# Issuing the next expert's input transposes ahead of, not behind, the current expert's first products in a mixture-of-experts tail

## The reference, cut to what matters

```
a_e = top2_idx.reshape(-1)                       # expert of each pick
keep = counts <= cap                             # cap = 320
buf = zeros((E, cap+1, H)).at[a_e, p].set(x_a)   # tokens sorted by expert
h = silu(einsum('ech,efh->ecf', buf, w1) + b1)   # 320 x 256 by 256 x 256, per expert
y = einsum('ecf,egf->ecg', h, w2) + b2           # the same again
```

## Time and profile before

| | us |
|---|---|
| runs | 1271.47, 1274.42, 1276.09 |
| median | 1274.42 |
| the profiled execution, its own time | 1271.47 |
| its span, first to last instruction | 1269.4 |
| mean granted clock of TensorE | 0.885 of full |

### The profile page before, as it was taken

The page is one execution under the profiler, slowest core; times in us unless marked ns, Lnnn a source line. Parts: engine busy times, 40 slices in busy tenths (PEclk is TensorE's granted clock), DMA queues, the critical chain, the costliest instruction groups (busy, mean ns, idle before and its releaser), DMA issues.

```text
span 1269.4 us, 19930 instructions
## 1 busy us (share of the span) xinstructions
PE 1015.9 (80%) x8500; PEld 763.2 (60%) x8500; DVE 579.0 (46%) x1328; ACT 356.8 (28%) x491; POOL 228.7 (18%) x234
## 2 busy tenths in 40 slices
PE   6989689989888888888875797888879797974860
PEld 3656566666657777787874564756556474643540
DVE  3544443544683421111113834655573659445227
ACT  2443323433441121111111243142315323330112
POOL 0310210210212223222221010101000110102642
PEclk9888888888988999999997996999699789965985
DMA  5012922012005787777762000200020010004426
GB/s 168 2 38 79 347 60 67 1 38 67 1 1 200 273 293 279 281 263 259 264 252 82 1 6 2 67 2 5 1 67 2 5 34 1 2 1 136 144 85 198
DMA packets 68216, 129.22 MB, mean 102 GB/s; under 512 B 12752, under 2 KB 57696, under 8 KB 63136
## 3 DMA queue, kind: packets, MB, share of 16 engines
q1 hardware_dynamic: 45984, 97.85, 22.6%
q10 hardware_dynamic: 16480, 14.62, 3.7%
q0 software_dynamic: 5664, 15.47, 3.4%
HBM read 94.50 MB, written 33.42 MB: 101 GB/s over the span
## 4 chain that ended last, share of the span: by engine, by line
PE 53%; DVE 22%; DMA 13%; ACT 6%; issue 2%; POOL 2%; SPq 1%; ACTq 1%; another core or an unknown queue 0%; POOLq 0%; DVEq 0%
DMA sb_arena<-in_m_w 10%; PE ps L1627 7%; PE ps L1324 6%; PE ps L1443 6%; DVE sb_arena L793 6%; PE ps L1509 5%; PE ps L1419 4%; ACT sb_arena L587 4%; DVE sb_arena L797 3%; PE ps L1637 3%; DVE ps L816 3%; PE ps L1562 2%; PE ps L1465 2%; PE ps L1701 2%; PE ps L1451 2%
## 5 line engine op out<-in xcount | busy, mean ns | idle before, releaser
L1627 PE MATMUL ps<-sb_arena 128*128 128x128 f32 x1248 | 160.0, 283 | 42.4 <-DMA sb_arena<-in_m_w 41.8
L1627 PEld LDWEIGHTS ps<-sb_arena 128*128 128x128 f32 x1248 | 149.8, 197 | 56.3 <-DMA sb_arena<-in_m_w 55.3
L1214 POOL TENSOR_TENSOR sb_arena<-sb_arena,sb_neghalf 128x2 f32<-128x2 f32 x40 | 30.4, 761 | 600.5 <-DVE sb_arena L759 600.5
L587 ACT ACTIVATE sb_arena<-ps 77x2048 f32<-77x2048 f32 (+1 forms) x64 | 118.5, 1874 | 54.7 <-PE ps L1401 42.8
L1324 PE MATMUL ps<-sb_arena,sb_wreg 128*128 128x256 f32 (+1 forms) x512 | 106.9, 361 | 4.6 <-issue 3.8
L1324 PEld LDWEIGHTS ps<-sb_arena,sb_wreg 128*128 128x128 f32 (+1 forms) x512 | 88.5, 194 | 19.4 <-issue 8.3
L1419 PE MATMUL ps<-sb_arena 32*77 32x256 f32 (+1 forms) x1024 | 93.8, 496 | 6.8 <-ACT sb_arena L587 4.0
L1112 DVE COPY sb_arena<-ps 128x256 f32<-128x256 f32 x39 | 16.5, 424 | 158.9 <-PE ps L1621 158.9
L822 DVE RECIPROCAL sb_arena<-ps 128x32 f32<-128x32 f32 x24 | 8.6, 357 | 147.3 <-PE ps L1451 146.4
L1637 PE MATMUL ps<-sb_arena 128*128 128x256 f32 x312 | 73.9, 380 | 0.6 <-ACT sb_arena L688 0.6
L1273 POOL DMA_INDIRECT outs<-sb_arena,sb_idx x39 | 38.3, 983 | 194.1 <-ACT sb_arena L688 194.1
(11 more groups left out here) (228 smaller groups left out, 1717.8 us busy)
## 6 DMA issues: line engine op xcount, KB each, us to landing
sb_arena<-in_m_w SPq DMA_DIRECT2D x39, 1536.0 KB
sent<-sb_xres SPq DMA_DIRECT2D x32, 256.0 KB, 2.9
sb_arena<-outs SPq DMA_DIRECT2D x16, 512.0 KB, 5.6
outs<-sb_zeros ACTq DMA_DIRECT2D x1, 6656.0 KB, 32.7
sent<-sb_zeros ACTq DMA_DIRECT2D x2, 2560.0 KB, 12.8
sb_arena<-in_m_w SPq DMA_DIRECT2D x16, 256.0 KB
early<-sb_xres SPq DMA_DIRECT2D x12, 256.0 KB, 2.9
sb_arena<-in_xT SPq DMA_DIRECT2D x8, 256.0 KB, 3.4
```

What stands on the lines that cost most here:

```text
L587: nc.scalar.activation(dst, src, ACT.Exp).then_inc(S(f"h_PT{p}"), 1)
L1214: g.tensor_tensor(b.rstd, b.var, neghalf[:, 0:NT], ALU.pow).then_inc(S(f"{n}_rstd{p}"), 1)
L1627: ins = mm(to[:, m * P:(m + 1) * P], w[:, k, m * P:(m + 1) * P], slots0[j % 2].xT[:, k, :], start=(k == 0), stop=(k == KC - 1))
```

## The change

Two lines move up within PE's loop over the experts. The transposes of expert `e + 1` are issued at the head of the loop body, ahead of the waits and first products of expert `e`. Nothing else differs: the same instructions, tiles, banks and semaphores, and the other four engines have the same instruction streams.

```
             turn1(0)
             for e in range(E):
                 b = experts1[e % XBUFS]
+                if e + 1 < E:
+                    turn1(e + 1)
                 pe.wait_ge(S(f"t_w{e % XBUFS}"), weights_at(e))
                 pe.wait_ge(S("e_xT"), e + 1)
...
                         ins = mm(ps[:, 2 + m, 0:CAP], b.w1[:, k, m * P:(m + 1) * P], xT1[:, k, CAP * e:CAP * (e + 1)],
                                  start=(k == 0), stop=(k == KC - 1))
                     ins.then_inc(S("e_u"), 1)
-                if e + 1 < E:
-                    turn1(e + 1)
                 pe.wait_ge(S("e_h"), KC * (e + 1))
```

## The result

| | before | the change |
|---|---|---|
| median of 22 runs each, us | 1274.91 | 1281.27 |
| lowest and highest | 1258.41 to 1284.74 | 1275.09 to 1286.59 |
| ratio, 95% interval | | 1.0066 (1.0044 to 1.0089) |
| the profiled execution, us | 1271.47 | 1270.34 |
| its span | 1269.4 | 1268.3 |

The change is slower, as forecast, but by more than forecast: 4.18 us would be 0.33%, and the ratio says 0.66%. By the medians the loss is 6.4 us, by the ratio 8.4 us. The profiled execution of the change, however, is 1.1 us faster than that of the kernel before. So the two profiles can't explain the difference of the medians. They can show what happened to each step.

The account below looks back on a forecast made before the run. PE, with 53% of the chain, was taken to bound the kernel. Bare transposes, 1.98 + 1.32 + 0.88 = 4.18 us, on the median 1274.42 gave 1278.6 us; range 1273.5 to 1282.5, the forecast's own 1276.5 to 1280.5.

Parts of the forecast that it names:

- The gap of the Silu: Between first and second products PE waits 0.62 us for the Silu, whether or not transposes stand there.
- The warm sets: Transposes of experts 2 to 7 laid bare at full clock: 3 x 0.66 = 1.98 us and 3 x 0.44 = 1.32 us.
- The cold set of expert 1: Four transposes ahead of expert 0's first products at half clock: 0.88 us, bounds 0.44 and 2.5 us.
- The moved waits: Waits for gathers and DVE's copy, moved with the transposes, cost nothing; tightest gather, expert 4's, has 2.4 us of slack.
- The clock: By the skill's rule the new 0.62 us gaps would be dear; the trace does not bear it out.
- The sum: Bare transposes of experts 1 to 7 together: 1.98 + 1.32 + 0.88 = 4.18 us slower, chance 0.60.
- the two long waits: Second products of experts 3 and 4 start 2.23 and 2.16 us late; with a cold set 5.97 us, left unchanged.
- rival 1: Late signals at experts 3 and 4 do not recur: saves 5.97, pays 4.18, so -1.8 us, 1272.6; chance 0.12.
- Rivals 3 and 4: 3: every new gap cools the clock, 26 us, 1300, chance 0.03. 4: transposes hide at new place, 1274.4, chance 0.09.
- Rival 2: One more cold stretch, at expert 3 or expert 0's start: 5.8 or 6.4 us, 1280.2 to 1280.8; chance 0.16.

Follow-up runs that it names:

- e1: The changed kernel with four unused transposes of the identity matrix in each gap ahead of the second products: ratio 1.0035 to the kernel before.
- e7: The kernel before with one transpose for each of experts 1 to 7 instead of six or four, at the old place: ratio 0.9991.
- p1: The kernel before with a short POOL addition, about 0.7 us, ahead of each gather in the loop: ratio 1.0009 to the kernel before.
- c1: The kernel before, unchanged, timed against itself and profiled a second time: ratio 1.0009.
- e4: The kernel before with PE one expert deeper (first products e + 1, transposes e + 2, second products e) and DVE reordered to match: ratio 1.0011.
- q: Pair q1 and q2, old and changed order with POOL quiet: the change costs 3.9 us by the ratios, 3.1 by the medians.
- p: Pair p1 and p2, old and changed order with POOL pauses: the change costs 3.6 us by the ratios, 2.5 by the medians.
- c3: The changed kernel, unchanged, measured once more against the kernel before: ratio 1.0022.
- c5: The changed kernel, unchanged, in the fourth batch against the kernel before: ratio 1.0047.
- c4: The changed kernel, unchanged, measured a fourth time against the kernel before: ratio 1.0014.
- e2: The kernel before with PE one expert deeper (first products e + 1, transposes e + 2, second products e), DVE's order left: ratio 1.0163, 21 us slower.
- q1: The kernel before with all 20 gathers ahead of POOL's loop and all scatters behind the last expert: ratio 1.0218.
- q2: The changed kernel with all 20 gathers ahead of POOL's loop and all scatters behind the last expert: ratio 1.0249 to the kernel before.
- g1: The kernel before with all 20 gathers ahead of POOL's loop, scatters left in the loop: ratio 1.0066.
- p2: The changed kernel with a short POOL addition, about 0.7 us, ahead of each gather in the loop: ratio 1.0037 to the kernel before.
- c2: The changed kernel, unchanged, in the first batch against the kernel before: ratio 1.0037.
- e3: The changed kernel with expert 1's transposes back behind the first products of expert 0: ratio 1.0011 to the kernel before.
- e5: The changed kernel with each set of transposes of experts 1 to 7 issued twice at the new place: ratio 1.0043 to the kernel before.

## Why the prediction was right and wrong

**The gap of the Silu.** Right: it is 0.62 us at experts 1 to 7 of the undisturbed change, and the same with four transposes in it (e1) or with one (e7).

**The warm sets.** Forecast 3.30 us. Between the second products of expert 0 and those of expert 7 the change takes 1225.75 - 1181.37 = 44.38 us, p1 1221.63 - 1180.41 = 41.22: 3.16 us. Six transposes cost 0.61 us where I took 0.66, four cost the 0.44 that I took.

**The cold set of expert 1.** Forecast 0.88 us. The second products of expert 0 start 8.34 us behind the first transposes, against 7.60 before and 7.59 in p1, but 8.01 in c1: 0.3 to 0.75 us. In the profile of the change the clock rose at about 1178.9, inside the first products, so these did not run cold to their end and took a part of it back.

**The moved waits.** Right: no idle time ahead of the transposes beyond DVE's copy at expert 0. The slack in the gathers is real but finite; the deeper order of e4 used it up.

**The clock.** The new gaps of 0.62 us lie at full clock, and no set behind them was slower. That such gaps would be dear was the prediction's own step from the rule that it named: the section of the Trainium skill (TensorE: Matmul & The Clock Gate, HAM oscillation) describes a loop in which each wait for a DMA is longer than the 2 us or so of matmuls ahead of it.

**The sum.** The undisturbed rows give 3.3 to 3.9 us, where the forecast was 4.18. By ratios, the pairs with an equal edit on POOL give 3.9 us (q) and 3.6 us (p), and the four later direct comparisons 1.8 to 6.0 us; by medians all of these are lower, 3.1, 2.5 and 0.8 to 4.9 us. So the mechanism and its size hold in the rows. The first measurement, 6.4 to 8.4 us, is one and a half times to twice the forecast. Its median of 1281.27 us still lies in the stated range, but by that range's width, which was drawn for late signals and cold sets, and not by the forecast's own, which ended at 1280.5.

**The step that failed** is in the passage on the two long waits: "so I leave this loss as it is". I took the 5.97 us of late signals as a fixed share of every execution of both kernels, and so as nothing in the sum. In the very next profile, that of the change, the loss was zero. That is the sign of rival 1, and the pair of profiles followed it (-1.1 us of span), but the medians did not. Profiles of the unchanged kernel had 6.0 us of it (57.81 against the 51.82 of p1) and then none (c1); profiles of the change had 0, 0, 4.1, 3.9 and 5.3 us. It also seems to come by batches. The medians of the kernel before were 1269.2 and 1270.0 us in the two batches whose profiles with POOL's usual or paced order have no late signals, and 1275.2 to 1278.0 us in the three with them. A term of the size of the whole effect, which comes and goes, should have widened the forecast's own range and not been set to cancel.

That late signals made the first 22 runs of the change worse by the missing 2.5 to 5 us is possible; it is not shown. What lifted that one measurement stays open. Two other sources of scatter are as large. Over all profiles the first transposes started between 1172.1 and 1179.7 us, behind the same PE code. And within one kernel the longer executions were mostly those with the lower granted clock: of the change, 1286.59 us at 0.875 and 1270.34 us at 0.892. The clocks of the kernel before in that first comparison are on record for the profiled execution only, so this can't settle it.

**The rivals.** Rivals 3 and 4 are out by the rows. Rival 1 came true in the pair of profiles and not in the medians. Rival 2 happened in part: where late signals came, sets of 4.28 and 4.65 us stood behind them in c3 and c5, and none in c4 or in the undisturbed profiles.

## What to carry to other kernels

Work that fills a wait has no price until it is moved: ask of each instruction what else could stand in its gap, and whether its new place has one. When an order is deepened, every engine that feeds it must be reordered with it, and its slack in transfers counted again. And a loss seen in one profiled execution is first to be looked for in a second one of the same kernel before it is added to or left out of a sum.

## What the runs showed of the hardware

Signals from TensorE to ScalarE and VectorE can arrive several microseconds late while GpSimd issues indirect DMAs on end. Thirteen profiles have the usual order of DMAs (all but e2, e4, q1, q2, g1, p1 and p2). In nine of them single sets of second products started late, after waits of 0.86 to 5.61 us. All stood at experts 2 to 5, and never at 6 and 7, where GpSimd pauses. With 20 gathers in a row the wait was 9.3 to 12.2 us (q1, q2, g1).

Unbroken issuing is not enough for it. In c1, c2, e1 and the profile of the change it lasted 28 us and nothing was late. Nor does the chip alone decide: the first two batches ran on the same one, the first without late signals in c1, c2 and e1, the second with them in c3, e3 and e5. Full DMA engines don't explain it either. Their mean busy share was 0.9 or more in eight of the 52 one-microsecond stretches from 1180 to 1232 us both in the disturbed kernel before and in the undisturbed c2, while it was 0.18 to 0.58 in the first part of q1's wait, from 1190 to 1196. No run parts the issuing on GpSimd from the transfers that it starts, and the mechanism was not found.
